# GpSimd's residual DMAs put right behind the numerator's, and ScalarE's last product evacuation put one step earlier

## The reference

```python
ekv, ek = exp(min(k, 30)) * k, exp(min(k, 30))
a = a * decay + ekv_t;  b = b * decay + ek_t      # scan, forward and in reverse
euk = exp(min(u + k, 30))
num = nf + nb - ekv + euk * k
den = df + db - ek + euk
base = sigmoid(x) * (num / max(den, 1e-8)) * (0.8 + 0.2 * tf)
bw = where(weight >= 0, 1, -1) * mean(|weight|, axis=1)
out = x + einsum('bsi,oi->bso', base, bw) + bias
```

## Time and profile before

| what | us |
|---|---|
| median of 3 runs | 544.06 (543.01 to 545.19) |
| the profiled execution | 544.33 |
| its span, first to last instruction | 542.6 |
| VectorE busy | 504.8 (93%) |
| ScalarE busy | 378.4 (70%) |
| TensorE matmul busy | 363.8 (67%) |
| GpSimd busy | 362.3 (67%) |

### The profile page before, as it was taken

The page is one execution under the profiler, slowest core; times in us unless marked ns, Lnnn a source line. Parts: engine busy times, 40 slices in busy tenths (PEclk is TensorE's granted clock), DMA queues, the critical chain, the costliest instruction groups (busy, mean ns, idle before and its releaser), DMA issues.

```text
span 542.6 us, 5454 instructions
## 1 busy us (share of the span) xinstructions
PE 363.8 (67%) x1803; PEld 224.1 (41%) x1803; DVE 504.8 (93%) x385; ACT 378.4 (70%) x415; POOL 362.3 (67%) x194
## 2 busy tenths in 40 slices
PE   2233333322578786786786798778799888759996
PEld 1123333312335544444443454554455444524442
DVE  4999999999999999999999999999999999994593
ACT  2849688585859697796969696978889595953100
POOL 0157676667677877777877788877877879873200
PEclk9975655556698798798899878878899999779999
DMA  6745677777633798788899788888779998982942
GB/s 192 196 136 175 195 185 182 206 200 194 155 97 102 148 194 173 163 206 160 157 192 194 153 177 182 185 185 180 180 134 193 216 200 148 195 169 65 185 164 117
DMA packets 125778, 92.64 MB, mean 171 GB/s; under 512 B 2844, under 2 KB 117560, under 8 KB 125752
## 3 DMA queue, kind: packets, MB, share of 16 engines
q0 software_dynamic: 30720, 33.56, 39.2%
q1 hardware_dynamic: 92952, 57.70, 36.0%
q10 hardware_dynamic: 2080, 1.05, 0.7%
HBM read 58.74 MB, written 16.78 MB: 139 GB/s over the span
## 4 chain that ended last, share of the span: by engine, by line
DVE 59%; issue 22%; PE 11%; POOL 5%; DVEq 1%; ACT 1%; DMA 1%; SPq 0%; ACTq 0%
DVE pair L683 25%; DVE pair L704 9%; DVE wkv L740 7%; DVE own L722 6%; POOL wkv L345 5%; DVE pair L721 4%; DVE pair L715 4%; PE sT L420 3%; PE kT L420 3%; PE yT L420 2%; PE prod L420 1%; DVE euk L745 1%; PE cols L420 1%; DVE y_start L696 1%; DMA cond<-in_cond_dram 1%
## 5 line engine op out<-in xcount | busy, mean ns | idle before, releaser
L385 PE MATMUL prod<-acts,sgn 128*128 128x512 f16 x768 | 181.3, 390 | 4.3 <-ACT orow L618 4.0
L704 DVE TENSOR_TENSOR_SCAN pair<-cols,y_start,pair 128x1024 f32<-128x1024 f32 x64 | 150.1, 2346 | 1.1
L363 PE MATMUL kT<-ident,k_nat 128*128 128x128 f32 x256 | 52.1, 371 | 147.1 <-DVE own L722 147.1
L683 DVE TENSOR_TENSOR_SCAN pair<-cols,pair 128x1024 f32<-128x1024 f32 x64 | 142.8, 2272 | 0.0
L326 POOL TENSOR_TENSOR wkv<-euk,rec 128x1024 f32<-128x1024 f32 x31 | 73.1, 2357 | 84.0 <-ACT rec L558 84.0
L385 PEld LDWEIGHTS prod<-acts,sgn 128*128 128x128 f16 (+1 forms) x768 | 77.4, 101 | 90.2 <-issue 9.6
L363 PEld LDWEIGHTS kT<-ident,k_nat 128*128 128x128 f32 x256 | 42.1, 192 | 158.5 <-issue 157.9
L556 ACT ACTIVATE rec<-euk,lnb 128x1024 f32<-128x1024 f32 x32 | 36.8, 1150 | 84.9 <-DVE euk L745 84.8
L335 POOL TENSOR_TENSOR wkv<-wkv,rec 128x1024 f32<-128x1024 f32 x31 | 72.9, 2350 | 18.1 <-ACT wkv L591 18.1
L345 POOL TENSOR_TENSOR wkv<-wkv,pair 128x1024 f32<-128x1024 f32 x31 | 74.1, 2392 | 11.5 <-DVE wkv L740 10.1
L301 POOL TENSOR_TENSOR acts<-wkv,rec 128x1024 f16<-128x1024 f32 x31 | 73.2, 2363 | 9.5 <-ACT rec L567 9.5
(11 more groups left out here) (88 smaller groups left out, 502.2 us busy)
## 6 DMA issues: line engine op xcount, KB each, us to landing
x_nat<-in_x_dram SPq DMA_DIRECT2D x32, 512.0 KB, 6.9
pair<-own POOLq DMA_DIRECT2D x32, 512.0 KB, 4.7
k_nat<-in_fside_BxSxS_dram SPq DMA_DIRECT2D x30, 512.0 KB, 3.5
o_nat<-in_x_dram POOLq DMA_DIRECT2D x24, 512.0 KB, 9.1
out_dram<-o_nat SPq DMA_DIRECT2D x24, 512.0 KB, 5.0
y_fm<-in_L_ffn_weight_dram SPq DMA_DIRECT2D x8, 512.0 KB, 5.7
x_end<-in_x_dram SPq DMA_DIRECT2D x6, 512.0 KB, 5.1
x_end<-in_L_ffn_bias_dram POOLq DMA_DIRECT2D x6, 512.0 KB, 6.0
```

The costliest lines, as they stand in the source:

```text
L363: ins = pe.transpose(dst(q), what(q), one)
L385: ins = pe.matmul(prod[:, h, :], view[:, c, m % CT * P:m % CT * P + P], acts[:, part, m // CT % 2 * CT + c, h * H:(h + 1) * H], start=(par ...
L683: dve.tensor_tensor_scan(buf, d, buf, 0.0, ALU.mult, ALU.add).then_inc(st["F" + kind], 1)
L704: dve.tensor_tensor_scan(buf[:, ::-1], d, buf[:, ::-1], y_start[:, i:i + 1], ALU.mult, ALU.add)\
```

## The change

In GpSimd's step all residual DMAs of the step and its bias DMA are issued right behind the numerator's DMA, ahead of the wait for `rec`. cleared(30) becomes 48, so that ScalarE evacuates unit 47 and copies unit 46 at the end of step 30. It copies unit 47 in step 31, behind `inverse(30)` and `halves(29)` and ahead of the wait for `chk`, where before the copy stood behind the steps. In TensorE's list the early part of product 8 is cut from six channel tiles to five, and moves ahead of the wait for `lo` of tile 29; the sixth is made with the rest of product 8 at the end.

```diff
     def cleared(n):
-        return 0 if n < LAG else made(n) - 1 if n < N - 1 else 2 * LAST
+        return 0 if n < LAG else made(n) - 1 if n < N - 2 else 2 * LAST
@@ gpsimd step
                     done(pool, "yn", n - 1)
                     pool.dma_start(ekv[1 - p], own[1 - p][:, :], accum_op=ALU.add).then_inc(num_in[1 - p], 16)
+                residuals(summed(n))
+                if 3 <= n <= TT:
+                    biases(n - 3)
+                if mid:
 
                     done(pool, "rec", n - 1)
                     done(pool, "lo", n - 3)
...
-                if not first:
-                    residuals(summed(n)[:1])
...
-                residuals(summed(n) if first else summed(n)[1:])
-                if 3 <= n <= TT:
-                    biases(n - 3)
@@ tensor, behind the steps
                 across(v, bank[v], range(CT - 3), True, False)
+            done(pe, "yc", 2 * LAST - 1)
+            across(8, bank[4], range(CT - 3), True, True).then_inc(st["early"], 1)
             done(pe, "lo", N - 3)
             for v in range(4):
                 across(v, bank[v], range(CT - 3, CT - 2), False, False)
-            done(pe, "yc", 2 * LAST - 1)
-            across(8, bank[4], range(CT - 2), True, True).then_inc(st["early"], 1)
             s_turn(N - 1)
...
-                tiles = range(CT - 2, CT) if v < 6 or v in (8, 9) else range(CT - 1, CT) if v < 8 else range(CT)
+                tiles = range({6: CT - 1, 7: CT - 1, 8: CT - 3}.get(v, CT - 2) if v < 10 else 0, CT)
@@ scalar step
                     clear(cleared(n - 1), made(n - 1))
+                if n == N - 1:
+                    y_copy(2 * LAST - 1)
                 if mid:
...
             run(None, step)
 
-            y_copy(2 * LAST - 1)
             early_out(0)
```

## The result

The changed kernel took 546.79 us (median of 4 runs, 546.53 to 547.49) beside 543.87 of the kernel before: ratio 1.0054, with a 95% interval of 1.0031 to 1.0077. That is 2.9 us slower, where 7.9 us faster were forecast. The profiled execution took 547.49 us, with a span of 545.7, 3.1 above the span of before.

What follows compares the result with a forecast made beforehand. It took VectorE's list in the steps and TensorE's in the tail as the bound. Gains of 3.1 (L745) and 4.9 (tail) make 8.0, so 544.33 becomes 536.3, given as 536.2 us; range 533.5 to 547.

Steps and rivals of the forecast that it cites:

- What bounds the kernel: Whole kernel: time is won only in VectorE's list in the steps and TensorE's list behind them.
- The room for the residuals on GpSimd: GpSimd's gap ahead of L326 takes in the moved issues, even two residuals (4.08 us); costed at nothing.
- Rival B: Steps 27 and 29: second back-to-back residual waits some 9 us for descriptor room; 550 us, chance 0.03.
- L745 and the second residual, 3.1 us: Steps 27 and 29: L345 starts earlier, so L745 waits 0.6 instead of 2.1; gain 3.1 us.
- The unknown term: VectorE's L715 beside the moved issues: wait between nothing and 1.43 us a step, taken as nothing.
- rival A: L715 waits for the DMA issue: full price 570.3 us, chance 0.18; a part, 537.5 to 547, chance 0.13.
- The bias issues, 4.1 us in rival A: L715 waits for bias issues too, in 6 steps, 0.87 - 0.19 each: 4.1 us of the full price.
- The tail, 4.9 us: TensorE's tail: unit 47's turn starts at 476.6 instead of 481.38, end at 533.2 instead of 538.02; gain 4.9 us.
- Rival C: The tail doesn't follow: TensorE held longer or clock stays at half, half of 4.9 lost; 538.7 us, chance 0.08.
- Rival D: Steps 27 and 29 keep L745's whole wait, another GpSimd instruction in the way: 539.3 us, chance 0.04.

Runs made afterwards that it cites:

- pairs_split: Kernel before plus ScalarE's and TensorE's edits; only in two-residual steps, one residual goes behind numerator's DMA and clamp, the other between chk and inv: 535.70 us, ratio 0.9846.
- den_wait: Changed kernel, but GpSimd waits for L745 of the tile before, then issues residual and bias DMAs: 536.49 us, ratio 0.9855.
- stt_clamp: Changed kernel with L715 written as a scalar_tensor_tensor, same result: 549.47 us (one run).
- few_pieces: Changed kernel with each residual's 512 KB read in 128 pieces instead of 1,024 (other elements of x): 536.38 us (one run).
- tail_only: Kernel before with only the ScalarE and TensorE half of the change, GpSimd's step as before: 539.23 us, ratio 0.9911.
- scalar_half: Kernel before with ScalarE's edit alone (unit 47 evacuated in step 30, copied in step 31): 542.21 us, ratio 0.9963.

## Why the prediction was wrong, point by point

- **What bounds the kernel**: right. All that changed did so through VectorE's list in the steps and TensorE's in the tail.
- **The room for the residuals on GpSimd**: right. `chk` still waits for `rec` in the ordinary steps. Two issues back to back take 3.46 us (421.82 to 425.28), the sum of 1.88 and 1.58, and `chk` starts right behind them, 4.35 behind the numerator's start where 4.08 were reckoned; the rest is L715's doing. Rival B falls. Here is step 27 of the changed kernel, 3.75 us for both from a printed start that is early by 0.3.

```profile
420.93 0.89 POOL L322 DMA_DIRECT2D pair<-own  x1
421.52 3.75 POOL L314 DMA_DIRECT2D o_nat<-in_x_dram  x2
424.44 3.23 POOL L330 TENSOR_TENSOR wkv<-euk,rec 128x1024 f32<-128x1024 f32 x1
```

- **L745 and the second residual, 3.1 us**: right in mechanism and, without L715's wait, in size: `pairs_split` kept 0.55 of wait in two steps. In the changed kernel all 4.3 went. The trace fits this reading: L715's wait sets VectorE back, so GpSimd is no longer late and `base` waits for `gate` again (0.30 at 433.91 in step 27); `den_wait`, with the same issues and no wait of L715, has the 0.55 again.
- **The unknown term**: this is the step that failed: L715's wait for the residual's issue was taken at nothing, and it is 0.575 us in each of 21 steps, 12.1 us. "No row shows a DMA issue beside L715" was right, and the two ends, 0 and 1.43, hold the measured value between them. I took 0 because "the nearest row is a DMA issue too (L322)". That row was a DMA issue of 128 pieces beside an instruction of another form, and `stt_clamp` and `few_pieces` show that each of these two differences alone takes the wait away. The nearness was in the name. The argument against rival A (most of the first 0.8 us of the issue may be no writing) would fit what 128 and 512 pieces do, and not 1,024.
- **Rival A**: the right mechanism at a size between its cases. Its full price (1.43 a step, 570 us) isn't there, since VectorE is let in within the issue; its part was cut off at 0.4 a step for no reason from a row, though the point from which it decides, 0.30, lay well inside the two ends. (That point was reckoned over 27 steps; the six with a bias DMA cost L715 nothing, so it is 8.0 / 21 = 0.38.) By the measured 0.575 its sum is 536.2 + 12.1 = 548.3, less the 1.2 us more that L745 gave: 547.1, and 546.79 was measured. Neither case covered 547 to 570. That the result lies just inside the range, whose end of 547 came from at most 0.4 in 27 steps, is luck: it was 0.575 in 21, with 1.2 back from L745. Of the rule named with it (the Trainium skill, SBUF — State Buffer, section Who interferes with whom), the traces here agree with two parts: the tensor_scalar is held up by an issue and the scalar_tensor_tensor at its place is not (`stt_clamp`), and the order matters (`den_wait`). They don't agree with the holder keeping the pair for the whole instruction, as L715 began 0.17 us into an issue and ended at 238.78, 0.39 before it.
- **The bias issues, 4.1 us in rival A**: that cost isn't there; the issue waits instead, and VectorE loses 0.04 a step at L689.
- **The tail, 4.9 us**: right, by the steps that were given for it where the tail stands alone; in the changed kernel the same 4.9 came with its waits in other places. Rival C falls. The clock behind a gap of 3.8 us was missed in an experiment's expectation.
- **Rival D**: falls, as both long instances of L745 are gone or shorter in every kernel that moves the second issue.

## What to carry to other kernels

A gap on GpSimd is not free for a DMA issue: look at what VectorE does beside it, and keep long issues (many pieces) off the start of VectorE's fast tensor_scalar forms; here the clamp waited 12.1 us in all when it started 0.17 us behind the issue, and not at all 0.38 us ahead of it, and one more wait of GpSimd (`den_wait`) turned a loss of 2.9 into a gain of 7.7. Where a cost lies between two bounds that no row narrows, work out the point at which it decides before taking an end, and leave no hole between the cases. A change of two halves is worth being timed in halves: the one gave 4.7, and the other hid it.

## What the runs showed of the hardware

- A GpSimd DMA issue of 1,024 pieces of 512 B holds up a VectorE tensor_scalar of 0.745 us that starts 0.17 us into it by 0.575 us, and one that starts 1.07 us into it by 0.29 us; one that started 0.38 us ahead of it isn't held. With 512 pieces of 1 KB, 0.17 us into the issue, it is 0.03 us, with 128 of 4 KB nothing, and the issue is longer instead (0.87 becomes 1.09 for a bias DMA). Why 512 pieces leave VectorE free where 1,024 don't stays open; that an issue of 1,024 holds VectorE up in two parts would fit both waits, and was not tried.
- GpSimd's issue of a DMA of 512 KB took 0.87 us with 128 pieces and 1.59 us with 1,024, and two of 1,024 back to back took 3.46 us, beside a median of 9.1 us from issue to landing: the second didn't wait for the first to land.
- A scalar_tensor_tensor of 1,024 float32 in the same place isn't held (1.218 us in the median, 1.226 at most).
- TensorE's granted clock was full (1.00) behind gaps of 1.44 us (`tail_only`) and 1.69 us (the changed kernel). Behind a gap of 3.82 us it was 0.53 over the next 3.55 us (`scalar_half`), with 8 matmuls in 3.34 us instead of 1.73, and behind one of 5.70 us it was 0.58 over the next 4.9 us (before). Half the clock would be 0.50.
